# Expert outputs gated at their copy-out and written to token rows by index, low parts on VectorE, and plain row loads in mixing

## The reference, cut to what matters

```python
xn = _layernorm(x)                                   # 4096 x 256
logits = xf @ Wg                                     # xf = xn as rows; 8 experts
top_vals, top_idx = jax.lax.top_k(softmax(logits), 2)
loc = ...                                            # place in the expert's queue
keep = loc < C                                       # C = 1280 places per expert
gates = top_vals * keep; gates = gates / gates.sum(-1)
buf = zeros((E, C + 1, h)).at[e_flat, l_flat].set(xk)
inp = buf[:, :C]
hid = einsum('ech,ehf->ecf', inp, W_in)              # 256 -> 2 x 512
a, g = split(hid, 2)
hid = gelu(a) * g
out_e = einsum('ecf,efh->ech', hid, W_out)           # 512 -> 256
gathered = out_pad[e_flat, l_flat]                   # both places of a token
y = (gathered * gates[..., None]).sum(axis=1)
x = x + attention0(xn) + y                           # attention0 ends with @ Wout + bout
xn = _layernorm(x)
# layer 1: sparsemax attention to 32 patterns in each of 16 heads, and an MLP of 8
# routed experts (2 chosen) and a shared one; x = x + attention1(xn) + ffn1(xn)
```

## Time and profile before

| | us |
|---|---|
| three runs | 2150.52, 2140.54, 2154.29 |
| median | 2150.52 |
| profiled execution | 2144.84 |
| its span, first to last instruction | 2143.1 |
| experts | 1068.8 to 1442.2 |
| mixing | 1442.2 to 1570.2 |
| layer 1 | 1570.2 to 2096.6 |

### The profile page before, as it was taken

One profiled execution on the slowest core, in us unless ns is written; L12 is line 12 of the kernel. 1 busy time (PEld: TensorE's weight loads), 2 busy tenths in 40 slices (PEclk: granted clock), 3 DMA queues, 4 the chain that ended last, 5 costly groups with the idle time before them and its releaser, 6 DMA issues. The chain is left out here.

```text
span 2143.1 us, 35073 instructions
## 1 busy us (share of the span) xinstructions
PE 1966.0 (92%) x11874; PEld 1195.0 (56%) x11874; DVE 1531.1 (71%) x3473; ACT 1035.6 (48%) x2246; POOL 514.3 (24%) x932
## 2 busy tenths in 40 slices
PE   6869999999999999999799999986678999999998
PEld 3333333333333333333299999984556777777776
DVE  7879988888888888888054333325578998889883
ACT  3426677676767777777744444432331122221112
POOL 4554123322222222222233333336400000000000
PEclk9979999999999999999999999998789999999998
DMA  6555111111101111110133222215410000000005
GB/s 206 183 160 200 62 38 58 56 38 40 35 32 38 41 43 43 43 43 11 52 101 100 90 84 88 90 42 163 144 51 12 9 21 20 20 20 20 10 11 162
DMA packets 111781, 143.69 MB, mean 67 GB/s; under 512 B 12153, under 2 KB 96769, under 8 KB 111233
## 3 DMA queue, kind: packets, MB, share of 16 engines
q1 hardware_dynamic: 87248, 98.09, 14.3%
q0 software_dynamic: 10400, 31.47, 4.4%
q10 hardware_dynamic: 13968, 12.06, 1.8%
HBM read 85.10 MB, written 56.10 MB: 66 GB/s over the span
## 5 line engine op out<-in xcount | busy, mean ns | idle before, releaser
L854 ACT ACTIVATE at_wt<-at_B 128x512 f32<-128x512 f32 (+3 forms) x1280 | 607.3, 538 | 257.7 <-PE at_B L953 240.8
L1259 DVE TENSOR_REDUCE at_piece_max<-at_A 128x1 f32<-128x512 f32 x768 | 489.0, 684 | 71.3 <-PE at_A L934 61.8
L971 PE MATMUL at_O<-at_wt,at_v 128*32 128x512 f32 (+3 forms) x2560 | 313.9, 543 | 0.0
L754 POOL TENSOR_SCALAR_AFFINE_SELECT at_wt<-at_wt 128x128 f32<-128x128 f32 x512 | 147.8, 294 | 632.6 <-ACT at_wt L854 623.9
L1256 DVE CUSTOM_DVE_ANT_0 at_junk<-at_A,s_hide 128x128 bf16<-128x128 f32 (+3 forms) x512 | 230.5, 487 | 69.6 <-PE at_A L934 69.0
L1474 PE MATMUL ex_H<-ex_xT,ex_w_in 128*128 128x256 f32 x1920 | 247.8, 286 | 4.0 <-DVE ex_xT L1581 4.0
L1474 PEld LDWEIGHTS ex_H<-ex_xT,ex_w_in 128*128 128x128 f32 x1920 | 237.0, 193 | 4.4 <-DVE ex_w_out L1586 4.4
L1595 DVE TENSOR_TENSOR ex_h<-ex_act_a,ex_H 128x256 f32<-128x256 f32 x160 | 66.8, 417 | 212.7 <-ACT ex_act_a L1523 212.6
L2170 ACT ACTIVATE l_act_g<-l_G 128x512 f32<-128x512 f32 x80 | 47.9, 599 | 305.9 <-PE l_G L2084 241.3
L934 PE MATMUL at_A<-s_k,s_q 96*128 96x512 bf16 (+2 forms) x480 | 165.7, 363 | 22.3 <-PEq L104 9.6
L1516 POOL TENSOR_TENSOR ex_hT<-ex_h,ex_hT 128x256 fp32r<-128x256 f32 x160 | 123.1, 774 | 254.3 <-ACT ex_hT L1527 254.3
(11 more groups left out here) (275 smaller groups left out, 2798.9 us busy)
## 6 DMA issues: line engine op xcount, KB each, us to landing
buf<-at_room POOLq DMA_DIRECT2D x10, 1024.0 KB, 8.7
s_first_rows<-buf SPq DMA_DIRECT2D x40, 256.0 KB, 2.7
expert_out<-ex_y ACTq DMA_DIRECT2D x40, 256.0 KB, 2.2
s_raw_in<-in_W_in SPq DMA_DIRECT2D x8, 1024.0 KB
q_parts<-parts SPq DMA_DIRECT2D x16, 384.0 KB, 3.5
s_down<-in_x SPq DMA_DIRECT2D x8, 512.0 KB, 4.7
xn<-s_raw_in SPq DMA_DIRECT2D x8, 512.0 KB, 5.4
at_v<-v SPq DMA_DIRECT2D x16, 256.0 KB, 3.0
```

Of the source, the lines that this page charges most:

```text
L754: pool.affine_select(block_, block_, [[1, P]], ALU.is_ge, 0.0, base=0, channel_multiplier=-1).then_inc(hidden, 1)
L854: act.activation(wt[(HP * p + h) % NE_][:, q0:CH], pB_of(p, h, u)[:, q0:CH], ACT.Exp, scale=D ** -0.5).then_inc(wt_ready, 1)
L971: pe.matmul(pO[j % 2][rows, q0:CH], vs[n % 3][:, kt // TPC, kt % TPC, :], wt[(HP * p + h) % NE_][:, q0:CH], start=kt < 2 and not late, sto ...
L1259: ins = dve.tensor_reduce(top, pA[slot % NA][:, 0:w], AX.X, ALU.max)
```

## The change

- A row of `buf` gets four more numbers: the token, the token's second expert, and its two gates. POOL copies them beside the row with four small copies per dispatch, and dispatch waits until the gates are there. Blank rows carry a token far out of range.
- `expert_out` is now in the order of tokens: rows 0 to 4095 for the first expert of a token, the next 4096 for the second. POOL zeroes it in attention with eight 1 MB transfers. `slot_get` goes.
- In experts, DVE works out from the loaded rows where each goes and which gate applies (five operations on 128x2 per tile) and makes the low parts of the hidden values. ACT's copy of the output becomes two activations of 128x256 that scale by the gate. POOL writes each by an indexed transfer; rows out of range are dropped. The last tile's writes are issued in mixing. The loops of DVE and SP are unrolled.
- In mixing, SP waits for all writes and then loads whole rows; DVE adds two 128x512 tiles instead of four gated 128x256 ones. The bias is loaded later.
- The score matrix of layer 1 goes out to memory in attention, comes back in mixing and is cut there. In layer 1 the scores are three products of parts (six matmuls of 128x512); DVE makes the columns' low parts (two of 128x512 per chunk); ACT gathers each half of the columns in one copy.
- Some semaphores are merged, `seg` is halved, `mixed` lies in two buffers, and finish's DVE loop is unrolled.

```diff
+                if n == 0:
+                    sp.wait_ge(act_step, at_act["to_scores1"])
+                    sp.dma_start(d["scores_raw"], scores_raw[:]).then_inc(pats_in, 16)
+            sp.wait_ge(pats_in, 32)
...
+                if n == 0:
+                    pool.wait_ge(routing_in, 48)
+                    pool.tensor_copy(token[:, :, 1], expert[:, 1]).then_inc(token_set, 1)
+                    pool.wait_ge(token_set, 2)
+                if n >= 2:
+                    pool.wait_ge(put[n % 2], 16 * 2 * TOPK * (n // 2))
                 for w in range(2):
-                    for c in (2 * n + w, TILES + 2 * n + w):
+                    pool.tensor_copy(xrow[n % 2][w][:, 0:E + 2:E + 1], token[:, 2 * n + w]).then_inc(token_set, 1)
+                    pool.tensor_copy(xrow[n % 2][w][:, E + 2:E + 4], gates[:, :, 2 * n + w]).then_inc(token_set, 1)
+                for w in range(2):
+                    pool.wait_ge(token_set, 4 * n + 2 * w + 4)
+                    for k in range(TOPK):
+                        c = k * TILES + 2 * n + w
...
             for n in range(HPAIRS):
                 for p in range(NPC):
                     if n == 0 and p % 4 == 0:
-                        pool.dma_start(blanks[p // 4], zeros.unsqueeze(1).to_broadcast([P, 8, E])).then_inc(buf_blank, 16)
+                        pool.dma_start(blanks[p // 4], zeros.unsqueeze(1).to_broadcast([P, 8, E + 4])).then_inc(buf_blank, 16)
+                    if p == 0 and 6 <= n < 6 + NO_ROWS:
+                        pool.dma_start(no_rows[n - 6],
+                                       zeros[:, 1:E + 1].unsqueeze(1).to_broadcast([P, 8, E])).then_inc(buf_blank, 16)
...
+                        pool.wait_ge(route_step, GATES_READY)
...
+                wait(sp, target_ready, 5 * (m - 1))
                 sp.dma_start(x[i], one(rows_in, m)).then_inc(x_loaded[i], 16)
...
-            with pool.Fori(0, ROUNDS) as j:
-                for i in range(PAIR):
-                    for f in range(FC):
-                        pool.wait_ge(h_high, FC * (PAIR * j + i) + f + 1)
-                        pool.tensor_tensor(hT[i % 2][1][:, f, :], h[i % 2][:, f, :],
-                                           hT[i % 2][0][:, f, :].bitcast(F32), ALU.subtract).then_inc(h_low, 1)
+            def store(m, t):
+                if t == 0:
+                    pool.wait_ge(target_ready, 5 * m + 2)
+                    pool.wait_ge(y_ready, RT * (m + 1))
+                pool.indirect_dma_start(
+                    out=d["expert_out"], out_offset=bass.IndirectOffsetOnAxis(ap=target[m % 8][:, t:t + 1], axis=0),
+                    in_=y[m % 2][:, t, :], in_offset=None, bounds_check=TOPK * NT - 1, oob_is_err=False,
+                ).then_inc(y_stored[m % 2], 16)
+
+            for m in range(LAST):
+                for t in range(RT):
+                    store(m, t)
...
+            def keep(m, i, u):
                 act.wait_ge(y_made, m + 1)
-                wait(act, y_stored[i], 16 * (m // 2))
-                act.copy(y[i][:], pY[i][:]).then_inc(y_ready, 1)
-
-            def store(m, i):
-                act.wait_ge(y_ready, m + 1)
-                act.dma_start(one(rows_out, m), y[i][:]).then_inc(y_stored[i], 16)
+                act.wait_ge(target_ready, 5 * m + 5)
+                to = s["last_y"] if isinstance(m, int) and m == LAST else y[i]
+                if to is y[i]:
+                    wait(act, y_stored[i], 16 * RT * (m // 2))
+                for t in range(RT):
+                    act.activation(to[:, t, :], pY[i][:, t, :], ACT.Identity, scale=gate[u][:, t:t + 1]).then_inc(y_ready, 1)
...
-                            keep(m - 1, 1 - b)
-                        if f == 2 and not (first and i == 0):
-                            store(m - 1, 1 - b)
+                            keep(m - 1, 1 - b, (i - 1) % GATES)
...
-            keep(PAIR * ROUNDS - 1, 1)
-            store(PAIR * ROUNDS - 1, 1)
-            for i in range(2):
-                act.wait_ge(y_stored[i], 16 * (PAIR // 2 * ROUNDS))
+            act.wait_ge(divided, TILES // 2)
+            keep(LAST, 1, LAST % GATES)
...
+            def find_target(m, u):
+                dve.wait_ge(x_loaded[u % 2], 16 * (m // 2 + 1))
+                wait(dve, y_stored[u % 2], 16 * RT * (m // 2 - 3))
+                dve.tensor_scalar(second[u][:], x[u % 2][:, :, E + 1], float(m // PER), float(NT), ALU.is_equal,
+                                  ALU.mult).then_inc(target_ready, 1)
+                dve.wait_ge(target_ready, 5 * m + 1)
+                to = s["last_target"] if m == LAST else target[u][:]
+                dve.tensor_tensor(to, second[u][:], x[u % 2][:, :, 0], ALU.add).then_inc(target_ready, 1)
+
+            def find_gate(m):
+                rows, halves, e = x[m % 2], gate_k[m % 2], float(m // PER)
+                dve.wait_ge(x_loaded[m % 2], 16 * (m // 2 + 1))
+                wait(dve, y_ready, RT * (m - GATES + 1))
+                wait(dve, target_ready, 5 * (m - 1))
+                for k, is_ in ((0, ALU.not_equal), (1, ALU.is_equal)):
+                    dve.scalar_tensor_tensor(halves[k][:], rows[:, :, E + 1], e, rows[:, :, E + 2 + k], is_,
+                                             ALU.mult).then_inc(target_ready, 1)
+                dve.wait_ge(target_ready, 5 * m + 4)
+                dve.tensor_tensor(gate[m % GATES][:], halves[0][:], halves[1][:], ALU.add).then_inc(target_ready, 1)
...
+            def low(m, b, f):
+                dve.wait_ge(h_high, FC * m + f + 1)
+                dve.tensor_tensor(hT[b][1][:, f, :], h[b][:, f, :], hT[b][0][:, f, :].bitcast(F32),
+                                  ALU.subtract).then_inc(h_low, 1)
...
+                        if f == 1 and not (last and i == PAIR - 1):
+                            find_target(m + 1, (m + 1) % 8)
+                        if f == 3 and not (last and i == PAIR - 1):
+                            find_gate(m + 1)
                         if f == 2:
                             cuts(cut, j, i, last)
+                        if f:
+                            low(m, b, f - 1)
+                        if f == FC - 1:
+                            low(m, b, f)
                         if f == FC - 1 and first:
                             divide(i)
...
+            def load_rows(t):
+                wait(sp, sums, SUMS * (t - NR + 1))
+                for k in range(TOPK):
+                    sp.dma_start(ye[k][t % NR][:], ye_rows[k][t]).then_inc(rows_in[t % NR], 16)
+
             for t in range(NR):
                 load(t)
+            for i in range(2):
+                sp.wait_ge(s["y_stored"][i], 16 * SLOTS // P // 2)
+            for t in range(NR):
+                load_rows(t)
+            sp.dma_start(lb_bias[:], d["lb_bias"].rearrange("(o n) -> o n", o=1).to_broadcast([P, NX])).then_inc(raw_in, 16)
+            sp.dma_start(scores_raw[:], d["scores_raw"]).then_inc(raw_in, 16)
...
+                    load_rows(t + NR)
...
-            for t in range(STEPS):
-                wait(pool, sums, SUMS * (t - NR + 1))
-                for k in range(TOPK):
-                    for w in range(2):
-                        c = k * TILES + 2 * t + w
-                        pool.indirect_dma_start(
-                            out=ye[k][t % NR][:, w, :], out_offset=None, in_=d["expert_out"],
-                            in_offset=bass.IndirectOffsetOnAxis(ap=s["slot_get"][:, c:c + 1], axis=0),
-                        ).then_inc(rows_in[t % NR], 16)
+            for w in range(2):
+                pool.indirect_dma_start(
+                    out=d["expert_out"], out_offset=bass.IndirectOffsetOnAxis(ap=s["last_target"][:, w:w + 1], axis=0),
+                    in_=s["last_y"][:, w, :], in_offset=None, bounds_check=TOPK * NT - 1, oob_is_err=False,
+                ).then_inc(s["y_stored"][1], 16)
...
-            pe.wait_ge(consts_in, 32)
             turn(0)
+            pe.wait_ge(consts_in, 16)
...
+                if t == SPLIT_AT:
+                    act.wait_ge(raw_in, 32)
+                    act.copy(s["to_scores0"][:], scores_raw[:])
...
-                    dve.wait_ge(rows_in[r], 64 * (t // NR + 1))
-                    for w in range(2):
-                        dve.scalar_tensor_tensor(part[u][:, 1, w], ye[0][r][:, w], s["gates"][:, 0, 2 * t + w:2 * t + w + 1],
-                                                 part[u][:, 0, w], ALU.mult, ALU.add).then_inc(sums, 1)
+                    dve.wait_ge(rows_in[r], 16 * TOPK * (t // NR + 1))
+                    dve.tensor_tensor(part[u][:, 1], ye[0][r][:], part[u][:, 0], ALU.add).then_inc(sums, 1)
...
-                    dve.wait_ge(sums, SUMS * t + 3)
+                    dve.wait_ge(sums, SUMS * t + 2)
...
-                    for w in range(2):
-                        dve.scalar_tensor_tensor(x1[r][:, w], ye[1][r][:, w], s["gates"][:, 1, 2 * t + w:2 * t + w + 1],
```

(20 more changed lines are left out.)

155 lines of the change are left out of this document (94 added, 61 removed).

## The result

The changed kernel took 2088.33 us (median of 5, 2084.36 to 2092.38), the kernel before 2149.55 us beside it. The ratio is 0.9719, interval [0.9696, 0.9742]: 61 us or 2.8% less, against a forecast of 2108 (−37) with a range of 2090 to 2144. The sign was right, and mixing was rightly named as the main place.

What follows compares the result with a forecast made beforehand. PE was taken to bound attention, experts and layer 1, and late signals beside gathers to hold mixing. From 2144.8 us, 0 + 3 − 2 − 30 − 7 + 1 − 2 = −37 gave 2108, range 2090 to 2144.

Steps and rivals of the forecast that it cites:

- Attention: 0 (from −2 to +3): Attention: POOL's added tiny copies and zeroing transfers cost nothing, its engine being far from full; 0 us, from −2 to +3.
- Mixing, the holds: −30: Mixing: plain loads replace gathers and remove 35.4 us of late PE signals, 5 kept back; −30 us, from −35 to 0.
- Mixing, the step: −7: Mixing: two plain DVE additions replace four gated ones, 0.5 us a step over 15 steps; −7 us, from −9 to −5.
- the +1 of the sum: Mixing: splitting the score matrix there, an ACT copy and a DVE subtraction once each; +1 us.
- Experts: +3: Experts: DVE takes the low parts, mostly under PE's cover, a few miss; +3 us, from 0 to +15.
- From experts to mixing: −2: Between experts' last output and mixing's first addition: a shorter chain to the first row load; −2 us, from −5 to 0.
- Layer 1: −2: Layer 1: split score products save PE 3 us, DVE's first low parts cost 1; −2 us, from −8 to +6.
- B: Rival, mixing: the holds stay with plain loads, being due to traffic and not its kind; 2138 us, chance 0.15.
- C: Rival, experts: indexed writes hold PE's signals as gathers did in mixing; +43 to +101 us, chance 0.08.
- D: Rival, experts: DVE's low parts are late for PE's output; +20 us, at worst +53, chance 0.10.
- E: Rival, mixing: row loads start late or bind, SyncE waiting for all stores; +5 to +15 us, chance 0.07.
- within 1%: Whole kernel: the case that the time stays within 1% (21 us) of the kernel before; chance given as 0.21.

Runs made afterwards that it cites:

- e10: The kernel before with four small POOL copies and their waits ahead of each dispatch's four indexed writes, on a chip with holds: 2138.19 us, ratio 0.9936.
- e11: The kernel before with the eight 1 MB zeroing transfers in attention and POOL's wait for them, on a chip with holds: 2144.28 us, ratio 0.9983.
- e9: The kernel before with mixing's 64 gathers replaced by 32 plain loads (index left out), on a chip with holds: 2111.41 us, ratio 0.9820.
- e2: The kernel before, unchanged, traced again on a chip without holds: 2097.54 us, ratio 0.9992.
- e6: The changed kernel with mixing's rows fetched by 64 POOL gathers in place of 32 plain loads: 2132.77 us against e5's 2089.44.
- e5: The changed kernel, unchanged, run again on a chip with holds: 2089.44 us, ratio 0.9735 to the kernel before.
- e14: The changed kernel, unchanged, run again on a chip without holds: 2080.94 us, ratio 0.9915 to the kernel before.
- e18: The changed kernel with each attention dispatch from the fifth pair of heads on written in two halves, second tile twelve pieces later, with holds: 2081.32 us, ratio 0.9630.
- e7: The changed kernel with the low parts of the hidden values made by POOL again, beside its indexed writes: 2137.39 us, 48 us more than e5.
- e3: The kernel before with dispatch buffer rows of 1040 bytes instead of 1024, on a chip without holds: ratio 0.9998.
- e1: The kernel before with mixing's 64 gathers replaced by 32 plain loads (index left out), on a chip without holds: 2090.86 us, ratio 0.9964.
- e12: The kernel before with dispatch buffer rows of 1040 bytes instead of 1024, on a chip with holds: ratio 0.9998.

## Why the prediction missed, point by point

**"Attention: 0 (from −2 to +3)" failed**, and with it the range. Attention and its end gave 11.4 us. I had counted only what the edits add to POOL, as busy time, and took the 64 indexed writes for harmless, "with no wait over 2.0". That wait was a hold: without holds the longest is 1.3, and attention 17 us shorter. The longest wait is a poor measure of it all the same: it is 1.3 in the changed kernel too, where holds still cost 11 us (937 against 926). What counts is the sum over all dispatches. Two edits that I costed as additions worked the other way: the small copies shorten the holds (e10, 14 us), and the zeroing transfers, with the wait for them, shorten POOL's drain (e11, 4.6 us). The drain was in the trace, as some 5 us of nobody working between attention and experts (the stretch 1064.0 to 1068.8 that the earlier trace rows skips), and I never asked who ended it.

The starting point had a part in it as well: the sum began at the profiled execution, 4.7 us below the median of before, and the profiled execution after, 2092.38, lies inside the range. By stretches, though, 52.5 against 37 is a miss too, and attention is the largest part of it.

**"Mixing, the holds: −30"** was right in cause, 5 low in size. With plain loads alone the additions take 69.4 (e9), 35 less than 104, and the 5 that I kept back for the denser traffic were not needed. Not all of the 35 are holds: gathers take 73.5 where nothing holds (e2), so 30.5 are holds and 4 the gathers' own price. e9 and e6 show the cause from both sides.

**"Mixing, the step: −7"**: 4.03 to 4.19 us, from 4.41 to 4.57 (e9): 0.38 a step, 5.3 for the fourteen behind the first, so 2 short. The first step still took 5.95 and the one with the split 5.27, the +1 of the sum. Together the two terms measure −4.2 (69.4 to 65.2) for −6.

**"Experts: +3"** and **"From experts to mixing: −2"**: +1.1 and −3.8 in this pair, −3 together in every pair, for +1. The steady part is full, 160.00 of 160. Low parts cost 0.418 on DVE, for 0.45 assumed, and PE waited 1.8 us for one, the last.

**"Layer 1: −2"**: −0.7, less than the spread of traces (528.8 to 531.9 in kernels with the layer 1 of before). The price per tile was right (0.3 for 0.23), but the next wait, for DVE's result, takes back three quarters, and the start, with low parts ahead of which nothing runs, costs 1 of the 2 us that the chunks gain: the changed kernel is 51.1 us ahead where the block begins, 50.2 at the first of the eight reductions (1644.0 and 1593.8), and 52.3 at the last.

**Rivals.** B is refuted by e9. C asked for holds in experts from indexed writes: experts are equally long with holds and without (371.7 in e5, 371.5 in e14). Two writes per 9 us tile do no harm there, while four in a row in attention do; whether it is their number or the 3.2 us of cover that PE has in experts is open. D and E did not come: the additions run at their step, and no output but the last waits for DVE. The Trainium skill, page "SBUF — State Buffer", section "Who interferes with whom", says that a DVE instruction with two SBUF inputs contends with a GpSimd instruction that reads SBUF. Beside 78 indexed writes the low parts took 415 to 425 ns, the 48 that ran while POOL issued one 415 to 420, so that an indexed transfer is no such instruction here. The same section's "DMA never contends with a compute engine" is not contradicted in its wording: the transposes ahead of the longest wait ran in 0.60 us, as those without holds do. What was late were signals, and those it does not speak of. Three later transposes of the first trace took 1.06 us (at 1524, 1541 and 1551), where the granted clock was lower (0.59 from 1535 to 1540).

**The chances** have a slip: 0.15 + 0.02 and the thirds of C and D are 0.23, not 0.21, for "within 1%", and 0.05 are left for slower. It changes no term.

**What the change is worth** depends on the chip: 58 to 61 us where signals are held, 17 where not. A forecast from one trace had no way to know that; the trace could only say how much was held.

Open is why copies of 0.2 us ahead of the writes shorten the holds, what in a chip makes them, and why more transfers, or the wait for them, make POOL's drain shorter. Each was measured, none explained. Open too are the 2 us by which attention starts later in this pair: other traces of both kernels start at 118 to 121.

## What to carry to other kernels

Count the time in which an engine has finished and its follower has not started, per kind of transfer in flight; where it comes only beside indexed transfers of POOL, it is a cost of those. Try writes two and two before four in a row: in attention the stretch went from 937 us to 928 (e18). Compare kernels on one chip, or look first what the kernel before takes there. Look at who ends the gap between two blocks. Before giving indexed writes to POOL, take from it what the critical engine waits for (e7: 48 us).

## What the runs showed of the hardware

- Where the kernel before took 2147 us or more, ACT waited up to 15.5 us (e6) for signals of PE beside runs of gathers, in all five traces with gathers; where it took 2098, in neither of the two (e2, e3). Attention with its 64 indexed writes took 944 to 950 us in the kernel before with holds (its first trace, e11, e9) against 928 without (e2), and 937 against 926 in the changed one (e5, e14).
- POOL's drain at the end of attention took 7.76 to 7.78 us with the kernel before's transfers, with holds and without (first trace, e1, e2, e9, e10), 7.58 with rows of 1040 bytes (e3, e12), and 3.16 to 3.18 with eight more 1 MB transfers and POOL's wait for them. In the first trace no transfer was in flight then, and the last indexed write had been issued 27 us earlier.
- POOL issues one indexed write in 0.97 us, 1.3 from start to start.
